# Routed blocks of an expert layer: upper products two blocks ahead of the lower ones, a third buffer of halves, and the turns moved behind the lower products

## The reference, cut to what matters

```python
gate_scores = softmax(xf @ gate_w)
topk_scores, topk_idx = top_k(gate_scores, 2)
topk_scores = topk_scores / sum(topk_scores)
h = gelu(einsum('td,edf->etf', xf, w1) + b1[:, None, :])     # 128 -> 512, "upper product"
y = einsum('etf,efd->etd', h, w2) + b2[:, None, :]           # 512 -> 128, "lower product"
out = einsum('kt,ktd->td', topk_scores.T, y[topk_idx.T, tok])
```

## Time and profile before

| | |
|---|---|
| median of 3 runs | 1134.16 us (1132.31 to 1142.68) |
| the profiled execution | 1135.89 us, its span 1133.8 us |
| mean granted TensorE clock, whole span | 0.929 |
| PE busy over the span | 973.2 us (86%) |
| DVE | 869.5 us (77%) |
| ACT | 752.7 us (66%) |
| POOL | 406.3 us (36%) |
| routed blocks, first upper product to last lower product | about 933 to 1093 us |
| read back, sums, norm and store | about 1094 to 1134 us |

### The profile page before, as it was taken

The page is one execution under the profiler, slowest core; times in us unless marked ns, Lnnn a source line. Parts: engine busy times, 40 slices in busy tenths (PEclk is TensorE's granted clock), DMA queues, the critical chain, the costliest instruction groups (busy, mean ns, idle before and its releaser), DMA issues. The chain is left out here.

```text
span 1133.8 us, 28996 instructions
## 1 busy us (share of the span) xinstructions
PE 973.2 (86%) x10222; PEld 620.2 (55%) x10222; DVE 869.5 (77%) x2324; ACT 752.7 (66%) x1476; POOL 406.3 (36%) x572
## 2 busy tenths in 40 slices
PE   4999999977789999999999995898788748888884
PEld 2788887753444444444444442465565537777741
DVE  5988999836888999688999985688678567666634
ACT  2666666638788888888888780577555425666634
POOL 3544545423533000000000002236667665555543
PEclk9999999957999999999999997799889658999998
DMA  8223332000013000222222220001111022222226
GB/s 266 101 104 119 119 106 72 4 2 19 1 39 103 1 1 1 89 75 75 75 75 74 75 66 32 25 24 37 41 49 42 23 64 68 66 62 62 59 69 175
DMA packets 60220, 72.60 MB, mean 64 GB/s; under 512 B 8858, under 2 KB 36764, under 8 KB 60080
## 3 DMA queue, kind: packets, MB, share of 16 engines
q1 hardware_dynamic: 51312, 60.05, 16.9%
q0 software_dynamic: 4544, 8.60, 2.3%
q10 hardware_dynamic: 4224, 2.10, 0.7%
HBM read 40.14 MB, written 31.49 MB: 63 GB/s over the span
## 5 line engine op out<-in xcount | busy, mean ns | idle before, releaser
L797 ACT ACTIVATE d__hf<-d__HB,dense__d 128x512 f32<-128x512 f32 x288 | 185.0, 680 | 40.0 <-PE d__HB L1023 39.0
L856 DVE TENSOR_TENSOR d__hl<-d__hf,d__hh 128x1024 f16<-128x1024 f32 x144 | 174.8, 1223 | 19.9 <-ACT d__hh L802 17.8
L802 ACT ACTIVATE d__hh<-d__hf 128x1024 f16<-128x1024 f32 x144 | 152.2, 1057 | 4.6
L770 POOL TENSOR_SCALAR d__rstd<-d__mv 128x4 f32<-128x4 f32 x16 | 14.7, 917 | 361.5 <-DVE d__mv L980 361.5
L1021 PE MATMUL d__YB<-d__hh,d__w2h 128*128 128x512 f16 x288 | 110.4, 383 | 3.2 <-DVE d__tmp L913 3.2
L1021 PE MATMUL d__HB<-d__xh,d__w1h 128*128 128x512 f16 x288 | 111.2, 386 | 0.0
L1022 PE MATMUL d__HB<-d__xl,d__w1h 128*128 128x512 f16 x288 | 110.9, 385 | 0.0
L1023 PE MATMUL d__HB<-d__xh,d__w1l 128*128 128x512 f16 x288 | 110.8, 385 | 0.0
L1022 PE MATMUL d__YB<-d__hl,d__w2h 128*128 128x512 f16 x288 | 110.4, 383 | 0.0
L1023 PE MATMUL d__YB<-d__hh,d__w2l 128*128 128x512 f16 x288 | 110.0, 382 | 0.0
L1275 POOL DMA_INDIRECT parts<-c__ys,c__dest x78 | 83.0, 1064 | 70.6 <-ACT c__ys L1302 39.2
(11 more groups left out here) (400 smaller groups left out, 2587.9 us busy)
## 6 DMA issues: line engine op xcount, KB each, us to landing
rows<-a__blank SPq DMA_DIRECT2D x72, 268.0 KB, 3.3
d__G<-gates SPq DMA_DIRECT2D x64, 256.0 KB, 3.1
c__xin<-rows SPq DMA_DIRECT2D x39, 134.0 KB
dense__stage<-e_w SPq DMA_DIRECT2D x16, 256.0 KB, 3.1
b__stage<-e_w SPq DMA_DIRECT2D x32, 128.0 KB, 2.3
c__yb<-parts SPq DMA_DIRECT2D x8, 256.0 KB, 8.3
c__yb<-parts ACTq DMA_DIRECT2D x8, 256.0 KB, 8.7
out<-c__xo SPq DMA_DIRECT2D x8, 256.0 KB, 2.3
```

Source lines behind the costliest of these rows:

```text
L797: act.activation(hf[:, q, f], HB[:, f], gelu, scale=1.0 / WS, bias=b1[:, at:at + 1]).then_inc(s_["h_free"], 1)
L802: act.activation(hh[:, j % (LEAD + 1), f - 1:f + 1], hf[:, q, f - 1:f + 1], ACT.Copy).then_inc(s_["hi_done"], 1)
L856: dve.tensor_tensor(hl[:, p, f], hf[:, q, f], hh[:, p, f], ALU.subtract).then_inc(s_["lo%d_done" % i], 1)
```

## The change

In all three streams the upper product, the gelu and the halves go two blocks ahead of the lower product in place of one, `hh` and `hl` have three buffers in place of two, and the turns of a block come behind the lower product (on ACT behind `weighed`), one block further ahead than before.

```diff
-    hh = [m.sb(f"hh{p}", [P, FB, BLOCK], F16) for p in range(2)]
-    hl = [m.sb(f"hl{p}", [P, FB, BLOCK], F16) for p in range(2)]
+    hh = [m.sb(f"hh{p}", [P, FB, BLOCK], F16) for p in range(3)]
+    hl = [m.sb(f"hl{p}", [P, FB, BLOCK], F16) for p in range(3)]
...
         hidden(0)
+        hidden(1)
+        act.wait_ge(s["gt_full"], 1)
+        act.activation(gts[:], GT, ACT.Copy).then_inc(s["gt_done"], 1)
+        turned(3)
         for b in range(NBLK):
             if b == MORE:
                 biases(1)
-            if b + 1 == EARLY:
+            if b + 2 == EARLY:
                 act.wait_ge(s["bias_done"], 2)
-            if b + 1 < NBLK:
-                hidden(b + 1)
-            if b == 0:
-                act.wait_ge(s["gt_full"], 1)
-                act.activation(gts[:], GT, ACT.Copy).then_inc(s["gt_done"], 1)
-            if b + 3 < NBLK:
-                turned(b + 3)
+            if b + 2 < NBLK:
+                hidden(b + 2)
             weighed(b)
+            if b + 4 < NBLK:
+                turned(b + 4)
...
         def halves(b):
-            p = b % 2
+            h, p = hf[b % 2], b % 3
             for i in range(2):
                 f = slice(2 * i, 2 * i + 2)
                 dve.wait_ge(s["gelu_done"], 2 * b + i + 1)
-                wait(dve, s["y_full"], b - 1)
-                dve.tensor_copy(hh[p][:, f], hf[p][:, f]).then_inc(s["high_own"], 1)
+                wait(dve, s["y_full"], b - 2)
+                dve.tensor_copy(hh[p][:, f], h[:, f]).then_inc(s["high_own"], 1)
...
         halves(0)
+        halves(1)
         table_counts(dve, 1)
         for b in range(NBLK):
-            if b + 1 < NBLK:
-                halves(b + 1)
             if b + 2 < NBLK:
+                halves(b + 2)
                 target(b + 2)
...
         def down(b):
-            p = b % 2
+            p = b % 3
...
         pe.wait_ge(s["gt_done"], 1)
-        down(0)
-        for b in range(1, NBLK):
+        for b in range(NBLK):
             if b == MORE:
                 pe.wait_ge(s["ys_done"], b - 1)
                 biases(1)
-            if b + 1 < NBLK:
-                hidden(b + 1)
-            if b + 3 < NBLK:
-                turned(b + 3)
+            if b + 2 < NBLK:
+                hidden(b + 2)
             if b == MORE:
                 pe.wait_ge(s["bias_done"], 2)
             down(b)
+            if b + 4 < NBLK:
+                turned(b + 4)
```

More of the change, by code:

```diff
@@ L1424, in halves @@
                 dve.wait_ge(s["gelu_done"], 2 * b + i + 1)
-                wait(dve, s["y_full"], b - 1)
-                dve.tensor_copy(hh[p][:, f], hf[p][:, f]).then_inc(s["high_own"], 1)
+                wait(dve, s["y_full"], b - 2)
+                dve.tensor_copy(hh[p][:, f], h[:, f]).then_inc(s["high_own"], 1)
                 dve.wait_ge(s["high_own"], 2 * b + i + 1)
-                dve.tensor_tensor(hl[p][:, f], hf[p][:, f], hh[p][:, f], ALU.subtract).then_inc(s["lo_done"], 1)
+                dve.tensor_tensor(hl[p][:, f], h[:, f], hh[p][:, f], ALU.subtract).then_inc(s["lo_done"], 1)
         return target, halves
```

## The result

The changed kernel takes 1142.53 us (median of 20 runs, 1134.75 to 1148.83), the kernel before beside it 1135.25 (20 runs). The ratio is **1.0061, 95% interval 1.0042 to 1.0079**: 4.8 to 9.0 us more on 1134.16, where I forecast 4.6 less. The profiled execution has a span of 1139.6 us against 1133.8.

What follows compares the result with a forecast made beforehand. The prediction took POOL's scatters holding PE's signals, a loop of 7.55 us per two blocks, as the bound. From 1134.2 us, -6.1 and +1.5 gave -4.6, forecast 1129 us; range 1109 to 1146, likeliest case 1122 to 1137.

Steps and rivals of the forecast that it cites:

- the loop of signal, `weighed`, scatters, signal: Routed blocks: PE's signal comes after POOL's scatters end; 7.55 us for two blocks, 4.42 us for one.
- the waits for low halves: PE's waits at the start of 17 lower products, 10.3 us in all; they go, worth nothing by themselves.
- The runs of two go: POOL, routed blocks: scatters of single blocks become pairs, 37 blocks in 139.7 us in place of 145.8, -6.1 us.
- D: Rival: half an upper product held, two activations (0.8 us) ahead of `weighed` each cycle; 1144 us, chance 0.10.
- C: Rival: PE crawls in the hold, POOL scatters one block at a time, 4.42 us each; 1153 us, chance 0.10.
- Turns behind the lower products: PE and ACT: they make a third block too late to join POOL's run; `turned` waits for nothing new.
- Biases and table: `table_rows` behind three blocks' halves, second span's biases ahead of upper product 7: 0 to +2 us each, taken 0.
- The start: ACT has block 2's four activations ahead of the first `weighed`, so POOL's first scatters begin later: +1.5 us.
- Third buffer: `halves` of block b+2 waits for the lower product of b-1, same distance in PE's work as before: nothing.
- DVE beside POOL: Scatters starting beside DVE casts take longer; no change taken, bounds +8.5 to -8.5 us.

Runs made afterwards that it cites:

- The plain transfers: POOL's two indirect scatters per block replaced by plain transfers from SP: 0.9695 on the changed kernel, 0.9696 on the kernel before.
- the gap: A POOL memset of 128 x 860 halves added behind each block's two scatters: 0.9913 on the changed kernel, 0.9957 on the kernel before.
- the early table: DVE's `table_rows` put right behind `table_experts`: 1.0058 on the changed kernel, 1.0041 on the changed kernel with `weighed(b)` ahead of `hidden(b + 2)`.
- the turns ahead: Changed kernel with the turns of block b + 4 put back ahead of the lower product on PE and ahead of `weighed` on ACT: 1.0061.
- `weighed` first: Changed kernel with ACT's `weighed(b)` put ahead of `hidden(b + 2)`, PE's order kept: 1.0041.

## Why the prediction was wrong

**Right:** what bounds the stage. POOL's runs of scatters hold PE's signals, and the loop of signal, `weighed`, scatters, signal sets the pace. The plain transfers (3.05 us a block) and the gap (3.24 us) show it. Also right: the waits for low halves go, and they are worth nothing by themselves. There was more to that than I saw: they are gone from the steady blocks when the scatters are.

**The step that failed** is "what they do is have the second block of each pair finished when the signal comes. The runs of two go", -6.1 us. I took PE's work ahead as a gain and did not ask what PE does inside the hold with it. Runs of two rose to 13, and blocks 8 to 20 alone took 4.3 us more. Two of the rivals' mechanisms acted together. D: the signal that is held is now the upper product's, and ACT meets its four activations ahead of `weighed`; I had half an upper product at 0.8 us, it was a whole one, 1.4 us. C: PE crawls in the hold, and the second lower product comes after POOL's two scatters. For C I wrote "Against it: PE runs further ahead than today"; running ahead did not keep PE from crawling. What I had no term for is the clock, some 3.4 us by the estimate above. In the steady stretch of the before trace it is 1.00, and I did not ask what would keep it there, though the fall stands in the same trace, at the transposes of the earlier trace rows and behind them:

```profile
943.00:946.00 3.00, 0.65 (x3) 0.29 (x3) 2.63 (x9) 0.00 (x0) 1.52 (x3) 0.94 0.15 49
946.00:949.00 3.00, 2.89 (x26) 2.76 (x27) 1.19 (x3) 2.67 (x8) 1.17 (x1) 0.50 0.00 0
```

That the lower clock follows from PE standing still is read from order in time, in three kernels (972 to 979, 953 to 959, and 943 to 949 in the kernel before), not tried by itself. It does not follow each time: in the changed kernel PE is busy for 0.87 of the 2.60 us from 1010.40 to 1013.00 and for 0.68 of the 2.60 us from 1066.40 to 1069.00, and the clock falls behind the first and stays 1.00 behind the second. The Trainium skill ("TensorE: Matmul & The Clock Gate", section "HAM oscillation — how this bites in real kernels") describes a kernel where PE waits for DMA between bursts of matmuls, and each burst after a wait starts at the lower rate. The three stretches with 0.50 agree with that, the one at 1069 does not. What decides stays open here.

**Turns behind the lower products**, taken at nothing: by themselves 1.0072. **Biases and table**, 0 to +2 us each, taken 0: blocks 0 to 8 took 1.6 us more, but the early table gave none of it back (34.3 us in its profiled execution), so the size may stand, but the cause is not the table. **The start**, +1.5 us: +0.8 (4.1 to 4.9). **Third buffer**: nothing was seen of it, and it was not tried by itself. **DVE beside POOL**, no change taken: the mean scatter went from 1067 ns to 1029 (below), 78 x 38 ns or 3 us less in all, an estimate; in the prediction's terms a gain, and too small against the runs of two. The group of the scatters in the changed kernel:

```profile
L1275 POOL DMA_INDIRECT parts<-c__ys,c__dest x78 | 80.3, 1029 | 78.4 <-ACT c__ys L1302 43.5 <-DVE c__gate L1419 17.6 <-issue 17.3
```

The range held the time; the chances leaned the wrong way, since C and D had 0.10 each as if they excluded each other.

What stays open: why PE stops inside the lower product (after 19 of its 24 matmuls at 972.34 and in the one from 984.45 on, later at 1023 and 1066); why the kernel with the turns ahead loses at the start and the end; and how the measured 0.4% of `weighed` first and 0.4% with the early table come about, when in their profiled executions the sum is 191.1 and 188.5 us against 190.1. A profiled execution is one of many, and where the pairs fall in it varies.

## What to carry to other kernels

Before giving an engine more work ahead, find out whether the wait that this removes is a cause: here it was a symptom of another engine's work, and the engine that ran ahead only stopped later, in some cycles going on at a lower clock. Where signals are held behind a queue's burst, look at which signal comes out first and what the in-order engine behind it does with it. A short pause in the bursting engine was worth more than any reordering.

## What the runs showed of the hardware

- Inside a run of scatters single signals of PE get through around the start of a scatter or in the pause of 0.3 to 0.4 us ahead of it: scatters at 970.43 and 971.98, ACT going on at 970.53 and 972.04 (above). In the two holds read closely ACT went on 0.78 and 0.87 us behind the run's last scatter (974.23 to 975.01, and 1013.92 to 1014.79 in the earlier trace rows).
- PE's signals wait for POOL's scatters; ACT's to POOL do not. In the kernel before `weighed` at 1017.20 falls into the run that starts at 1016.24, and POOL goes on from its second scatter to the third with a pause of 0.30 us.
- The memset on POOL holds up DVE. In the changed kernel with the gap a cast that takes 0.43 us elsewhere took 0.98 beside the memset of 1011.05 (above), and ended 0.28 us behind it. A `tensor_scalar` of 128 x 32, 0.24 us in the kernel with `weighed` first, took 1.58 us beside a scatter and the memset, and a cast took 1.75; both end within 0.3 us of the memset that ran beside them (946.57 to 947.41, 949.80 to 950.64):

```profile
945.87 1.58 DVE L1397 TENSOR_SCALAR c__inside<-c__inside,c__taken 128x32 f32<-128x32 f32 x1
...
949.18 1.75 DVE L1430 CAST c__hh<-c__hf 128x512 f16<-128x512 f32 x1 [0.22 <-DVE c__mine L1407]
...
1011.19 0.98 DVE L1430 CAST c__hh<-c__hf 128x512 f16<-128x512 f32 x1
```

The Trainium skill ("SBUF — State Buffer", section "Who interferes with whom") has a cast and a `tensor_scalar` among the operations that, in a two-port mode, can lock the ports shared with GpSimd, the one that comes first blocking the other for its whole instruction. The cast at 1011.19, which starts behind the memset and ends behind it, agrees. The other two start ahead of the memset, beside a scatter, and end behind the memset all the same; which of the two held them isn't shown.
